# Attention and feed-forward kernel: softmax units of 128 rows that cross the heads, in place of units of 112 rows

## What is computed

```python
sim = einsum('bihd,bjhd->bhij', q, k) * scale          # 224 x 750 per head and batch
sim = where(mask, sim, -max)
attn = softmax(sim, axis=-1)
out = einsum('bhij,bjhd->bihd', attn, v) @ W_o + b_o
x = x + tanh(g_xattn) * out
x = x + tanh(g_ffn) * bitlinear(gelu(bitlinear(layernorm(x), w1, b1)), w2, b2)
```

## Time and profile before

| | |
|---|---|
| median of 3 runs | 1063.77 us (1063.48 to 1067.22) |
| profiled execution, span from its first instruction to its last | 1062.5 us |
| PE busy | 1011.3 us, 95% |
| ACT, DVE, POOL busy | 846.1, 818.6, 765.7 us |
| DMA | 168.83 MB, mean 159 GB/s |
| granted TensorE clock | 0.997 of 2.4 GHz over the span |

### The profile page before, as it was taken

The page is one execution under the profiler, slowest core; times in us unless marked ns, Lnnn a source line. Parts: engine busy times, 40 slices in busy tenths (PEclk is TensorE's granted clock), DMA queues, the critical chain, the costliest instruction groups (busy, mean ns, idle before and its releaser), DMA issues.

```text
span 1062.5 us, 24267 instructions
## 1 busy us (share of the span) xinstructions
PE 1011.3 (95%) x8576; PEld 600.3 (56%) x8576; DVE 818.6 (77%) x1774; ACT 846.1 (80%) x1458; POOL 765.7 (72%) x743
## 2 busy tenths in 40 slices
PE   4989999999999999999999999999999999999877
PEld 2556555556555655656565566656555556566433
DVE  4697988868788777878868777887868767797866
ACT  4878686987969769796978878797896977789766
POOL 4498987677766778776776787777686687787751
PEclk9999999999999999999999999999999999999999
DMA  8599898886978888796887988788896799678760
GB/s 264 198 208 243 140 203 152 162 161 141 172 139 159 160 167 165 140 170 138 171 166 134 169 149 166 143 175 163 147 171 128 148 180 177 127 129 146 132 122 31
DMA packets 472135, 168.83 MB, mean 159 GB/s; under 512 B 450384, under 2 KB 452176, under 8 KB 471632
## 3 DMA queue, kind: packets, MB, share of 16 engines
q1 hardware_dynamic: 472016, 167.29, 80.8%
HBM read 48.09 MB, written 7.34 MB: 52 GB/s over the span
## 4 chain that ended last, share of the span: by engine, by line
PE 75%; POOL 8%; ACT 6%; DMA 5%; issue 3%; DVE 2%; SPq 0%; POOLq 0%; ACTq 0%; DVEq 0%
PE ps_g L647 41%; PE ps_s L677 10%; PE ps_g L704 9%; PE ps_g L743 7%; PE ps_g L780 7%; DMA pt<-p 4%; POOL p L1199 3%; PE ps_g L692 1%; POOL p L1194 1%; ACT prob L1042 1%; POOL ctx L1210 1%; ACT hq L1158 1%; ACT h_sb L1148 1%; ACT p L1049 1%; POOL attn L1205 1%
## 5 line engine op out<-in xcount | busy, mean ns | idle before, releaser
L1199 POOL TENSOR_TENSOR p<-prob,p 112x750 f16<-112x750 f32 x256 | 405.8, 1596 | 94.3 <-ACT p L1049 92.0
L862 DVE CUSTOM_DVE_ANT_0 prob<-ps_s,mbias 112x750 f32<-112x750 f32 x256 | 236.7, 936 | 63.0 <-PE ps_s L677 54.8
L1042 ACT ACTIVATE prob<-prob,rmin 112x750 f32<-112x750 f32 x256 | 232.7, 912 | 5.7 <-DVE rmin L862 5.3
L647 PE MATMUL ps_g<-ctx,wk 128*128 128x375 f16 x1152 | 200.8, 326 | 18.3 <-POOL ctx L1210 16.4
L647 PE MATMUL ps_g<-wv,ctx 128*128 128x512 f16 (+1 forms) x864 | 196.5, 379 | 0.0
L647 PEld LDWEIGHTS ps_g<-ctx,wk 128*128 128x128 f16 x1152 | 110.3, 98 | 101.1 <-issue 27.0
L677 PE MATMUL ps_s<-k_sb,q_sb 64*112 64x375 f16 x1536 | 149.8, 327 | 7.4 <-DVE rmin L862 7.4
L1049 ACT ACTIVATE p<-prob 112x750 f16<-112x750 f32 x160 | 127.9, 820 | 18.7 <-DMA pt<-p 18.1
L647 PEld LDWEIGHTS ps_g<-wv,ctx 128*128 128x128 f16 (+1 forms) x864 | 86.3, 103 | 94.4 <-issue 5.2
L704 PE MATMUL ps_g<-pt,v_sb 128*64 128x224 f16 (+1 forms) x2448 | 123.2, 255 | 9.2 <-DMA pt<-p 9.2
L677 PEld LDWEIGHTS ps_s<-k_sb,q_sb 64*112 64x112 f16 x1536 | 90.0, 126 | 60.0 <-issue 35.5
(11 more groups left out here) (134 smaller groups left out, 1462.4 us busy)
## 6 DMA issues: line engine op xcount, KB each, us to landing
ctx_f<-in_ctx SPq DMA_DIRECT2D x47, 375.0 KB, 3.9
xa<-in_x SPq DMA_DIRECT2D x16, 448.0 KB, 4.6
xr<-in_x SPq DMA_DIRECT2D x28, 256.0 KB, 3.0
out<-xr SPq DMA_DIRECT2D x28, 256.0 KB, 2.6
pt<-p SPq DMA_TRANSPOSE x256, 4.2
h_sb<-in_w SPq DMA_DIRECT2D x4, 512.0 KB, 8.3
w<-in_w SPq DMA_DIRECT2D x3, 512.0 KB, 5.4
xr<-in_w SPq DMA_DIRECT2D x3, 512.0 KB, 11.2
```

What stands on the lines that cost most here:

```text
L647: mm = nc.tensor.matmul(out, lhs, rhs, start=(m == 0), stop=(m == len(steps) - 1))
L862: nc.vector.tensor_tensor_reduce(prob[:, (b * NU + n) % PROBS, :].rearrange("p (c k) -> p c k", c=2), ps_s[0:HT, n % 2, :, 0:CH], mbias[:, ...
L1042: nc.scalar.activation(prob[:, (b * NU + n) % PROBS, :], prob[:, (b * NU + n) % PROBS, :], ACT.Exp, bias=rmin[:, n:n + 1], scale=-1.0, acc ...
L1199: nc.gpsimd.tensor_tensor(p16[:, u % HILO, 1, 0:J], prob[:, (b * NU + n) % PROBS, :], p16[:, u % HILO, 0, 0:J], ALU.subtract).then_inc(s[" ...
```

## The change

The 224 queries of the 4 pairs of heads are laid end to end (896 rows for each of the two heads of a pair, `e`), and cut into 7 units of 128 rows. Units 0, 2, 4 and 6 lie within one pair; units 1, 3 and 5 cross from one to the next (rows 96 + 32, 64 + 64, 32 + 96). Such a unit is made of tiles of equal width, 32 or 64 queries: 48 or 24 matmuls of 375 columns in place of 12, each into its own partitions of `ps_s`. `M`, `E`, `H`, `L` work on 128 partitions, 14 times a batch where it was 16.

`pt` becomes a ring of 448 rows; unit 3 lies across its end, so its transposes are cut in two. `rrec` moves out of `ps_s`, the bias is kept in bf16, `rb` goes (ACT writes the spread reciprocals into `att` and now waits for POOL's `attn_lo` of the PV before), the last batch is cut into parts of 96 and 128 queries, and `R` is an item of its own in DVE's order. All five orders are new, written out for every batch.

```diff
-NM = 2 * NP
-NU = 2 * H
+NM = NP * TQ // 128
+NU = 2 * NM
+FIRST_PART = 96
...
-TURNED = 3
+RING_ROWS = 2 * TQ
...
+def pieces_of(b, m):
+    out = []
+    for j in range(NP):
+        for _, q, size, at in rows_of(b, j):
+            start, stop = max(at, 128 * m), min(at + size, 128 * (m + 1))
+            if start < stop:
+                out.append((j, q + start - at, start - 128 * m, stop - start))
+    return sorted(out, key=lambda piece: piece[2])
...
+def turned_parts(b, m):
+    out, at = [], 0
+    while at < 128:
+        row = 128 * m + at
+        place = place_of_row(b, row)
+        size = min(128 - at, RING_ROWS - place)
+        end = row + size - 1
+        if b < LB or row < NP * FIRST_PART:
+            after = b * NP + (end - RING_ROWS) // TQ
...
-HI_ON_ACT = [n for n in range(NU) if n % 8 not in (2, 5, 7)]
+HI_ON_ACT = [n for n in range(NU) if n not in (2, 5, 7, 10, 12)]
...
-        mbias = sb("mbias", [HT, J], F32)
+        mbias = sb("mbias", [128, J], BF16)
...
-        rrec = ps_s[0:HT, 1, 1, 512 - NU:512]
+        rrec = sb("rrec", [128, NU], F32)
...
-        pt = sb("pt", [128, TURNED, 2, 2 * NT, HT], F16)
+        pt = sb("pt", [128, 2, 2 * NT, RING_ROWS], F16)
         att = sb("att", [128, TQ], F32)
-        rb = sb("rb", [128, TQ], F32)
...
-                    sp.dma_start_transpose(pt[:, place_of(b, n // 2), n % 2, :, :],
-                                           p16[:, u % HILO, :, :].rearrange("p a k -> p (a k)"))\
-                        .then_inc(d_turn[u % HILO], 16)
+                    for at, size, place, after in turned_parts(b, n // 2):
+                        need(sp, "weighted", 0, after)
+                        sp.dma_start_transpose(pt[:, n % 2, :, place:place + size],
+                                               p16[at:at + size, u % HILO, :, :].rearrange("p a k -> p (a k)"))\
+                            .then_inc(d_turn[u % HILO], 16)
...
                     need(pe, "row_min", b, 2 * n - 1)
+                    width = min(size for _, _, _, size in pieces)
+                    tiles = [(j, q + k, at + k) for j, q, at, size in pieces for k in range(0, size, width)]
                     terms = ((0, 0), (1, 0), (0, 1))
                     for c in range(2):
                         for m, (qa, ka) in enumerate(terms):
-                            for e in range(2):
-                                rows = slice(e * DH, (e + 1) * DH)
-                                mm = nc.tensor.matmul(ps_s[0:HT, e, c, 0:CH],
-                                                      q_sb[rows, j, qa, half * HT:(half + 1) * HT],
-                                                      k_sb[rows, j, ka, c * CH:(c + 1) * CH],
-                                                      start=(m == 0), stop=(m == len(terms) - 1))
+                            for j, q, at in tiles:
+                                for e in range(2):
+                                    rows = slice(e * DH, (e + 1) * DH)
+                                    mm = nc.tensor.matmul(ps_s[at:at + width, e, c, 0:CH],
+                                                          q_sb[rows, j, qa, q:q + width],
+                                                          k_sb[rows, j, ka, c * CH:(c + 1) * CH],
+                                                          start=(m == 0), stop=(m == len(terms) - 1))
                     mm.then_inc(s["scores"], 1)
...
                 elif kind == "R":
-
-                    need(dve, "row_min", LB, NU - 1)
                     take_reciprocals(b, n)
                 elif kind == "PA":
                     need(dve, "recips_out", b, n)
-                    need(dve, "attn_lo", b, 2 * n - 1)
-                    qs = slice(0, queries_of(b))
-                    nc.vector.tensor_tensor(att[:, qs], g[:, qs], rb[:, qs], ALU.mult)\
+                    qs = slice(0, queries_of(b, n))
+                    nc.vector.tensor_tensor(att[:, qs], g[:, qs], att[:, qs], ALU.mult)\
                         .then_inc(s["attn_raw"], 1)
...
-                    need(act, "attn_raw", b, n - 1)
-                    nc.scalar.activation(rb[:, 0:queries_of(b)], g[:, 256:256 + queries_of(b)], ACT.Copy, scale=1.0 / RS)\
+                    need(act, "attn_lo", b, 2 * n - 1)
+                    nc.scalar.activation(att[:, 0:queries_of(b, n)], g[:, 256:256 + queries_of(b, n)], ACT.Copy, scale=1.0 / RS)\
```

More of the change, by code:

```diff
@@ L286, with rows_of, last_unit, weighs @@
 }
-def taken_after(b, n):
-    if b == LB and n >= 4:
-        return [(b, n // 2 - 2)] if n % 2 == 0 else []
-    return [divmod(b * NP + (n - 6) // 4, NP)] if n % 4 == 2 and b * NU + n >= 6 else []
+def rows_of(b, j):
+    if b < LB:
+        return [(j, 0, TQ, j * TQ)]
+    return [(j, 0, FIRST_PART, j * FIRST_PART), (j, FIRST_PART, TQ - FIRST_PART, NP * FIRST_PART + j * (TQ - FIRST_PART))]
+def pieces_of(b, m):
[6 more added lines that the diff above has]
+    return sorted(out, key=lambda piece: piece[2])
+def last_unit(b, j):
+    return max(m for m in range(NM) if any(piece[0] == j for piece in pieces_of(b, m)))
+def weighs(b, n):
+    j, part = n % NP, n // NP
+    return rows_of(b, j)[part]
+def units_of(b, n):
+    _, _, size, at = weighs(b, n)
+    return list(range(at // 128, (at + size - 1) // 128 + 1))
+def place_of_row(b, row):
+    if b == LB and row >= NP * FIRST_PART:
+        return (row - NP * FIRST_PART) % (3 * 128)
+    return row % RING_ROWS
+def turned_parts(b, m):
[7 more added lines that the diff above has]
+            after = b * NP + (end - RING_ROWS) // TQ
+        elif m < NM - 1:
+            after = b * NP + (place + size - 1) // FIRST_PART
+        else:
+            after = b * NP + NP
+        out.append((at, size, place, after))
+        at += size
+    return out
+def turns_before(u):
+    return sum(len(turned_parts(v // NU, v % NU // 2)) for v in range(u % HILO, u + 1, HILO))
+def recips_units(b, n):
+    return slice(2 * n, 2 * n + 2) if b == LB else slice(4 * n, min(4 * n + 4, NU))
+def recips_for(b, n):
+    last = 2 * units_of(b, n)[-1] + 1
+    return last // 2 if b == LB else last // 4
 def emptied(kind, n, b):
@@ L697, in emit @@
+                    for m in units_of(b, n):
+                        for e in range(2):
+                            need_turned(pe, b * NU + 2 * m + e)
                     if n == 0:
                         need(pe, "v_lo", b, NT - 1)
-                    places = sorted(place_of(b, m) for m in units)
-                    both = slice(places[0], places[-1] + 1, max(1, places[-1] - places[0]))
+                    place = place_of_row(b, row)
                     steps = [(t, va, pa) for t in range(NT) for va, pa in ((0, 0), (1, 0), (0, 1))]
@@ L728, in emit @@
                     t = tile_of(b, n)
[L729 removed]
+                    need(pe, "attn_lo", b, 2 * (2 * NP if t == NR - 1 else NP) - 1)
                     at = t * ROWS % RINGQ
```

505 lines of the change are left out of this document (291 added, 214 removed).

## The result

The changed kernel takes 1105.57 us (median of 4 runs, 1103.81 to 1108.34), the kernel before in the same session 1063.62. The ratio is 1.0397, with a 95% interval of 1.0367 to 1.0426: 42 us slower, where 1045 us and a range of 1036 to 1066 were forecast. The profiled execution took 1108.3 us, its span is 1106.6.

A forecast was written before the change was run, and what follows sets the result against it. PE was taken to bound the kernel, busy 697.15 of 700 us from 200 to 900. Terms -22.0 + 1 + 1 - 2 + 3 + 1.5 - 1 = -18.5 us took 1063.8 to 1045 us, range 1036 to 1066.

The forecast's parts named there:

- the part on ACT, DVE and POOL: Fewer M, L, casts, E and H are hidden under PE in the long stretch; bf16 bias and separate `rrec` cost 0.
- the new orders: Rival: scores bunched around PV make PE wait for DVE at 16 places, 1057 us, up to 1062; chance 0.11.
- the wait of scores behind minima: PE's scores, PV, scores places go from 4 to 16, each waiting for DVE 0.27 us: +3 us, bounds 0 and +11.
- One unit a batch less and 32 fewer changes of form, -22: PE's work: 16 scores units of 1.19 us removed, -19.0, and 32 form changes of 0.10 us, -3.0.
- Crossing units at full rate, +1: Tiles of units of 24 and 48 matmuls work side by side; 0.03 us for each of 32 starts, +1 us.
- The floor on the rate: Rival: matmuls start no closer than about 0.024 us, lengthening units of 48, +6 to +8, 1052 us; chance 0.13.
- the slow column tiles: Third rival: four column tiles stream below full rate in the 32 units of 48, +31, 1076 us; chance 0.16, more 0.04.
- SP and the DMAs 0: Transpose queue: same turned numbers, 254 transposes for 256, covered by the ring of 448 rows: 0 us.
- Reciprocals +1: Reciprocals and PV on PE: 128 more short matmuls, between nothing and 3.5 us, taken as +1.
- Relief between 60 and 200 us, -2: From 60 to 200 us, with POOL less loaded, some of PE's 9.9 us idle goes: -2 us (0 to -5).
- The start, +1.5 (from -1 to +4): First matmul waits for context now asked for behind 768 KB of weights, mask and queries: +1.5 us.
- The end, -1: Last waits: one unit less, 96 queries to finish tile 26: -1 us (-4 to +2).

The follow-up runs named there:

- E9: Changed kernel, the two operations reading `rrec` replaced by two more reciprocals of the row sums, low part left out, orders kept: 1077.32 us.
- E1: Kernel before with one line changed, `rrec` in SBUF in place of the PSUM corner: 1095.57 us, ratio 1.0294.
- E2: Changed kernel with DVE's R items from batch 2 on moved between an even minimum and the odd one, `rrec` still in SBUF: 1142.58 us.
- E3: E2 with `rrec` of batches 2 to 15 back in the PSUM corner: 1104.82 us.
- E6: Changed kernel's 128-row units with the old orders (one unit a batch struck out), `rrec` in PSUM, third reciprocal group behind minimum 12: 1074.48 us.
- E7: E6 with `rrec` in SBUF: 1090.94 us, ratio 1.0265.
- E16: E12 with the high part of probability 13 in place of 12 copied by GpSimd, as in the old orders: 1056.92 us, ratio 0.9949.
- E8: Changed kernel with the first items of SP, ACT, POOL and DVE back in the old order, context first: 1109.22 us.
- E15: E9 with the first items of each engine in the old order, as in E8: 1082.00 us, ratio 1.0178.
- E12: E9 with the old orders (one unit a batch struck out) for the start and batches 2 to 11, the new ones after: 1063.26 us.
- E10: Kernel before with three reciprocals as in E9 and `rrec` in SBUF: 1061.93 us, ratio 0.9985.

## Why the prediction was wrong

The step that failed stands in the part on ACT, DVE and POOL: "The bf16 bias and the separate `rrec` I cost at 0; DVE, with 161 us to spare in the 700, covers them." The cover was the wrong one. What `rrec` in SBUF adds is no work but waiting, and each wait holds everything behind it on DVE, which runs in order. 0 should have been +28 (E9), and 16 to 38 by the other pairs (E1, E2 with E3, E6 with E7). The bf16 bias did cost nothing: a minimum takes 933 ns for 936.

The second miss is a rival with too small a price. I gave the new orders 0.11 and 12 to 17 us more than the forecast; they cost 20.4, 6.3 of it by the choice of the probability that GpSimd copies. I had looked for the wait of scores behind minima, and that term was right: between 100 and 960 us E9, free of the port, has 4.0 us of it, +3 was my term. The rest lies in single late items of many kinds (in the middle transposes of PV and of the feed-forward, low parts of k, none over 2 us) and, at the start, in a first context that PE waits for 7.3 us longer than in E16. With both prices put in, 1045 + 28.3 + 20.4 is 1094. The other 12 us are what E16, without either, is above the forecast: PE's work 13.7 us less where I had 20, and 6.9 us more idle time where I had 1.5.

Point by point:

- *One unit a batch less and 32 fewer changes of form, -22.* The mechanism holds. E16's PE work is 13.7 us less in all, 16.1 in the middle's ten batches, at a mean clock (0.989 for 0.997) that hides some.
- *Crossing units at full rate, +1.* Right: 1.08 us for 24 and for 48, forecast 1.09 to 1.15. The floor on the rate and the slow column tiles, 0.29 of chance together, are out. First to last start of 48 matmuls is 0.83 us, one in 0.018.
- *SP and the DMAs 0.* Right. PE waits 9.4 us for transposes, 9.2 before, and a transpose takes a median of 4.1 us for 4.2. *Reciprocals +1:* no run takes this term apart.
- *Relief between 60 and 200 us, -2.* Wrong sign in the changed kernel (PE idles 18.5 us for 9.9).
- *The start, +1.5 (from -1 to +4).* The first matmul comes at 22.61 us for 15.16, beyond the bound and beyond the 20 us that I had named as a sign of error. E8 and E15 show that mending this alone brings nothing.
- *The end, -1.* E9's last stretch is 3.6 us shorter than before's; E16's, with the same orders there, 2.7 longer.
- *The clock.* I wrote that nothing could be won back from it, and did not ask what could be lost. In the changed kernel's trace nine stretches of 3.41 or 6.83 us at the lower level start in or behind pauses of PE of 1.8 to 3.6 us, and they took back most of the work saved.

One figure in the chances doesn't come out: 0.56 + 0.13 + 0.04 is 0.73, and 0.75 adds 0.02 for "half of the third", which is half of no rival's chance.

Of my signs, the count and length of units and the means of M, E and L held; PE's idle between 200 and 900 us (31.5 for a limit of 12), the waits for `rmin` there (13.5 between 100 and 960, limit 5) and the first matmul said wrong.

Open: what E12 loses against E16, 6.3 us for which of two engines copies two of fourteen probabilities, is measured, and explained only in part. E12's start has 3.7 us more busy time of PE (189.9 for 186.2) at a mean clock of 0.95 for 0.98, and 1.6 us more idle time; why the pauses come there stays open. That GpSimd is what the operations wait for is read from the count of the long ones (all 67 start while it is busy) and from E10; no run took GpSimd's work away.

## What to carry to other kernels

Before costing a moved tile at nothing, list every instruction that reads it, with the engine, the number of its SBUF inputs and the neighbours on GpSimd: an operation of 160 ns in the path of an in-order engine can wait for another engine's instruction of 1.6 us, and sometimes for several. Spare time of an engine covers work, not waits. And a saving on a bounding engine that is full to 99.6% is kept only if the order stays as tight: here the new orders gave 20 us back, in the middle in pauses of under 2 us each.

## What the runs showed of the hardware

- A DVE operation that waits for GpSimd mostly gets in at the end of the instruction under way, but not always. 63 of the changed kernel's 67 long waits ended so. The one that began at 334.73 us waited for the end of five instructions, 6.25 us, though the first ended 0.65 us later. In E1, 14 of 86 waited for more than one.
- Of three DVE operations of the same size on small SBUF tiles, `reciprocal` keeps its 164 to 177 ns while `tensor_scalar` (f32 to f16) and `scalar_tensor_tensor` with two SBUF inputs rise to means of 495 to 870 (the changed kernel, E1, E2, E7).
- Eight tiles of 64 x 32 stream 375 columns each in the time of two of 64 x 128: 48 matmuls within 0.83 us of each other, 0.018 us apart.

The Trainium skill, TensorE: Matmul & The Clock Gate, section "Wait — 56ns, not 53.3ns?", has a floor of about 25 ns from start to start. By it, an estimate, a unit of 48 would take 1.20 us; the row has 1.08. The measurement decides: the floor does not hold across tiles.
